# A fused attention and feed-forward layer: the opening rewritten to work in tile pairs, with two more engines in the layer norm and extra unit-matrix matmuls

## What is computed

```
xn  = (x - mean(x)) / sqrt(var(x) + 1e-5)            # per row of 512
lin(a, w, s) = (a @ sign(w).T) * mean(|w|, row) * s
q, k, v = lin(xn, wq, sq), lin(xn, wk, sk), lin(xn, wv, sv)
att = softmax(q @ k.T / 4) @ v                        # 4 query heads share a k/v head
ffn = (silu(xn @ (gate*sg).T) * (xn @ (up*su).T)) @ (down*sd).T
out = x + lin(att, wo, so) + ffn
```

## Time and profile before

| | |
|---|---|
| time, median of 3 runs | 505.62 us (503.99, 505.62, 506.27) |
| span of the profiled execution | 502.6 us |
| TensorE busy in the span | 479.6 us (95%) |
| VectorE busy | 417.2 us (83%) |
| ScalarE busy | 350.3 us (70%) |
| GpSimd busy | 94.4 us (19%) |

### The profile page before, as it was taken

One profiled execution on the slowest core, in us unless ns is written; L12 is line 12 of the kernel. 1 busy time (PEld: TensorE's weight loads), 2 busy tenths in 40 slices (PEclk: granted clock), 3 DMA queues, 4 the chain that ended last, 5 costly groups with the idle time before them and its releaser, 6 DMA issues.

```text
span 502.6 us, 10338 instructions
## 1 busy us (share of the span) xinstructions
PE 479.6 (95%) x4186; PEld 163.0 (32%) x4186; DVE 417.2 (83%) x487; ACT 350.3 (70%) x655; POOL 94.4 (19%) x138
## 2 busy tenths in 40 slices
PE   0899999999999999999999999999999999999996
PEld 0564444434332222222222222222222233333442
DVE  6879868676778999999999999999999955223986
ACT  1853643343229999999999999999999978874000
POOL 4212334534323000000000000000000113241021
PEclk9999999999999999999999999999999999999999
DMA  8862782641103802102102211111120034452321
GB/s 260 252 123 81 159 171 38 187 91 22 23 0 42 148 23 63 40 24 65 39 25 63 40 37 49 41 53 32 41 62 24 14 96 107 110 148 79 105 82 45
DMA packets 31302, 39.02 MB, mean 78 GB/s; under 512 B 6608, under 2 KB 20816, under 8 KB 31256
## 3 DMA queue, kind: packets, MB, share of 16 engines
q1 hardware_dynamic: 22232, 27.34, 19.0%
q0 software_dynamic: 8304, 10.95, 11.8%
q10 hardware_dynamic: 720, 0.08, 0.1%
HBM read 33.24 MB, written 10.35 MB: 87 GB/s over the span
## 4 chain that ended last, share of the span: by engine, by line
PE 86%; ACT 8%; DVE 3%; issue 1%; DMA 1%; SPq 0%; ACTq 0%; DVEq 0%
PE ps L1301 25%; PE ps L1131 19%; PE ps L1235 12%; PE ps L1140 8%; ACT room L705 6%; PE ps L1207 5%; PE ps L1194 5%; PE ps L1110 3%; PE ps L1335 3%; PE ps L1271 2%; ACT osb L716 1%; DMA hlo<-x 1%; DVE nmx L838 1%; PE ps L1048 1%; PE ps L1102 1%
## 5 line engine op out<-in xcount | busy, mean ns | idle before, releaser
L838 DVE TENSOR_REDUCE nmx<-ps 128x1 f32<-128x1024 f32 x248 | 284.6, 1216 | 14.5 <-PE ps L1140 14.2
L705 ACT ACTIVATE room<-ps 128x512 f32<-128x512 f32 x512 | 272.4, 598 | 20.9 <-PE ps L1271 11.0
L1301 PE MATMUL ps<-room,vcur 128*32 128x256 f32 (+1 forms) x1880 | 159.1, 410 | 4.3 <-ACT osb L716 4.1
L1140 PE MATMUL ps<-kA,qst 48*128 48x512 f16 x496 | 140.4, 382 | 0.0
L1235 PE MATMUL ps<-qst,kB 50*128 50x512 f16 x432 | 132.2, 382 | 0.8 <-DVE room L937 0.5
L1131 PE MATMUL ps<-room,wf 128*128 128x512 f16 x448 | 100.6, 379 | 0.0
L1301 PEld LDWEIGHTS ps<-room,vcur 128*32 128x32 f32 x1880 | 37.1, 108 | 100.8 <-issue 55.6
L686 ACT ACTIVATE room<-ps,gsc 128x512 f32<-128x512 f32 x28 | 19.2, 687 | 61.6 <-PE ps L1131 61.6
L1131 PEld LDWEIGHTS ps<-room,wf 128*128 128x128 f16 x448 | 42.4, 98 | 55.1 <-issue 7.2
L1235 PEld LDWEIGHTS ps<-qst,kB 50*128 50x128 f16 x432 | 26.8, 93 | 89.1 <-ACT room L705 79.8
L543 POOL TENSOR_TENSOR hlo<-room,hhi 128x512 f16<-128x512 f32 x28 | 34.1, 1217 | 87.4 <-ACT hhi L616 87.4
(11 more groups left out here) (136 smaller groups left out, 320.1 us busy)
## 6 DMA issues: line engine op xcount, KB each, us to landing
qst<-q_scratch SPq DMA_DIRECT2D x32, 192.0 KB, 3.6
o_scratch<-osb SPq DMA_DIRECT2D x16, 256.0 KB, 2.3
q_scratch<-parts SPq DMA_DIRECT2D x12, 256.0 KB
hlo<-x SPq DMA_DIRECT2D x8, 256.0 KB, 6.1
parts<-x POOLq DMA_DIRECT2D x8, 256.0 KB, 3.5
wf<-gate POOLq DMA_DIRECT2D x14, 128.0 KB, 3.9
wf<-up POOLq DMA_DIRECT2D x14, 128.0 KB, 6.0
wd<-down POOLq DMA_DIRECT2D x1, 1792.0 KB, 14.3
```

Of the source, the lines that this page charges most:

```text
L705: nc.scalar.activation(probs[:, s % 2, r, :], ps[:, bank_of(gp, s, i), :], ACT.Exp, scale=gam_reg[par][r]).then_inc(scores_free, 1)
L838: nc.vector.tensor_reduce(nmx[:, hf, idx:idx + 1], bank_pair(idx % 2), AX.X, ALU.max, negate=True).then_inc(rows_free, 1)
L1140: return nc.tensor.matmul(ps[:, 2 * (idx % 2) + b, :], qst[low:low + KROWS, par, hf, head, qt * P:(qt + 1) * P], kA[low:low + KROWS, par, ...
L1301: mm = nc.tensor.matmul(ps[32 * r:32 * r + 32, 7, of], vcur[:, par, key_tile(r, j), :], probs[:, s % 2, r, of], start=(j == 0 and part == ...
```

## The change

It touches only the first two stages. Layer norm goes by pairs of tiles in place of groups of four. VectorE keeps the statistics, the reciprocal and the normalisation of tiles 6 and 7. GpSimd does the Newton step and a shift of minus mean times reciprocal, seven instructions per pair, six of which follow the reciprocal one after the other. ScalarE normalises tiles 0 to 5 with that scale and shift (new step `A`), and loads its SiLU table early (new step `U0`). The gain steps `K0` and `K1` go from the front of TensorE's list to behind `G0` and `P0`. TensorE's `U0` and `G1` go ahead of `S0` and `Z0`. The small vectors are laid side by side in one array on the host and come in one transfer on SyncE's queue behind wk, as `svb` does behind wv. The first feed-forward load is issued by GpSimd between its pairs 1 and 2. And TensorE does 24 float32 matmuls of the unit matrix with itself into bank 5, which nothing else uses then, before the first transpose, and two more after each of the transposes of tiles 0 to 5.

```diff
-    pe_order = ("K0 K1 X0 X1 X2 X3 X4 X5 X6 X7 G0 P0 P1 S0 Z0 U0 Z1 G1 P2 Z2 P3 U1 F2 F3 F4 P4 P5 F5 F6 A0 F7 A1 A2 "
+    pe_order = ("X0 X1 X2 X3 X4 X5 X6 X7 G0 K0 P0 K1 P1 U0 G1 S0 Z0 Z1 P2 Z2 P3 U1 F2 F3 F4 P4 P5 F5 F6 A0 F7 A1 A2 "
...
-    dve_order = ("M0 M1 J0 M2 J1 M3 H0 M4 R0 M5 N0 N1 M6 M7 L0 H1 N2 R1 N3 N4 L1 N5 L2 N6 N7 L3 L4 L5 L6 L7 J2 S0 Z0 "
+    dve_order = ("M0 M1 M2 R0 M3 M4 R1 M5 M6 R2 L0 M7 L1 R3 L2 N6 N7 L3 L4 L5 J0 L6 L7 J1 J2 S0 Z0 "
...
-    act_order = ("D0 C0 C1 D1 N1 C2 N2 C3 N0 C4 B5 C5 C6 C7 B4 B2 B0 B1 B3 F0 E0 E1 F1 X0 X1 F2 E3 F3 V2 W0 X3 F4 E4 E5 "
+    act_order = ("D0 A0 D1 A1 C0 D2 C1 A2 A3 D3 C2 A4 C3 A5 N0 C4 C5 C6 C7 N1 N2 U0 B5 B4 B2 B0 B1 B3 F0 E0 E1 F1 X0 X1 F2 E3 F3 V2 W0 X3 F4 E4 E5 "
...
-    NORM_GROUPS = [(0, 4), (4, 8)]
+    PAIRS = [(t, t + 2) for t in range(0, TT, 2)]
...
             load_weights(wk, NH * D, wk_loaded)
+            sp.dma_start(vec[:, :], vecs).then_inc(vec_loaded, 16)
             load_weights(wq, 0, wq_loaded)
             load_weights(wv, NH * D + KV, wv_loaded)
+            sp.dma_start(svb[:, :], sv.to_broadcast([P, KV])).then_inc(svb_loaded, 16)
...
-            pool.wait_ge(x_loaded[TT - 1], 16)
-            load_ffn(0)
...
+            for t0, t1 in PAIRS:
+                if t0 == TT // 2:
+                    load_ffn(0)
+                of = slice(t0, t1)
+                pool.wait_ge(stats_ready, t1)
+                step(nc.gpsimd.tensor_scalar(half_var[:, of], mv[:, of, 1], EPS, -0.5, ALU.add, ALU.mult))
+                pool.wait_ge(inverse_ready, t1 // 2)
+                step(nc.gpsimd.tensor_tensor(newton[:, of], rstd[:, of], rstd[:, of], ALU.mult))
+                step(nc.gpsimd.tensor_tensor(newton[:, of], newton[:, of], half_var[:, of], ALU.mult))
+                step(nc.gpsimd.tensor_scalar(newton[:, of], newton[:, of], 1.5, None, ALU.add))
+                step(nc.gpsimd.tensor_tensor(rstd[:, of], rstd[:, of], newton[:, of], ALU.mult))
+                step(nc.gpsimd.tensor_tensor(shift[:, of], mv[:, of, 0], rstd[:, of], ALU.mult))
+                nc.gpsimd.tensor_scalar(shift[:, of], shift[:, of], -1.0, None, ALU.mult).then_inc(rstd_ready, 1)
...
-            act.dma_start(gsc[:, :], sg).then_inc(gains_loaded, 16)
-            act.dma_start(usc[:, :], su).then_inc(gains_loaded, 16)
-            act.dma_start(scqk[:, 0:QT], sq).then_inc(vec_loaded, 16)
-            act.dma_start(scqk[:, QT:QT + 1], sk).then_inc(vec_loaded, 16)
...
-                    if n == 0:
-                        act.dma_start(svb[:, :], sv.to_broadcast([P, KV])).then_inc(vec_loaded, 16)
+                elif kind == "U":
+                    nc.scalar.activation(warm[:, :], eps[:, :], ACT.Silu)
+                elif kind == "A":
+                    act.wait_ge(rstd_ready, n // 2 + 1)
+                    if n >= 4:
+                        act.wait_ge(xT_ready, n - 3)
+                    nc.scalar.activation(xn[:, n % 4, :], xin[:, n, :], ACT.Identity, bias=shift[:, n:n + 1],
+                                         scale=rstd[:, n:n + 1]).then_inc(xn_act_ready, 1)
...
-                ln_result(nc.vector.reciprocal(rstd[:, of], std[:, of]))
-                ln_result(nc.vector.tensor_tensor(newton[:, of], rstd[:, of], rstd[:, of], ALU.mult))
-                ln_result(nc.vector.tensor_tensor(newton[:, of], newton[:, of], half_var[:, of], ALU.mult))
-                ln_result(nc.vector.scalar_tensor_tensor(out=rstd[:, of], in0=newton[:, of], scalar=1.5, in1=rstd[:, of],
-                                                         op0=ALU.add, op1=ALU.mult))
+                nc.vector.reciprocal(rstd[:, of], std[:, of]).then_inc(inverse_ready, 1)
...
+            def keep_warm(n_):
+
+                for _ in range(n_):
+                    nc.tensor.matmul(ps[:, 5, 0:P], ident[:, :], ident[:, :], start=True, stop=True)
+
+            keep_warm(24)
...
                 mm.then_inc(xT_ready, 1)
+                if i < TT - 2:
+                    keep_warm(2)
```

More of the change, by code:

```diff
@@ L25, with layer_kernel @@
 LIFT = 16384.0
-def layer_kernel(nc, x, wq, wk, wv, wo, wq_rows, wk_rows, wv_rows, wo_rows, sq, sk, sv, so, gate, up, down, sg, su, sd, out,
+def layer_kernel(nc, x, wq, wk, wv, wo, wq_rows, wk_rows, wv_rows, wo_rows, sv, so, vecs, gate, up, down, sd, out,
                  q_scratch, k_scratch, o_scratch, r_scratch):
@@ L74, in layer_kernel @@
     T_AT = [n for kind, n in pe_order[:pe_order.index(("T", 0))] if kind == "F"][-1]
-    NORM_GROUPS = [(0, 4), (4, 8)]
+    PAIRS = [(t, t + 2) for t in range(0, TT, 2)]
+    ACT_NORM = [n for kind, n in act_order if kind == "A"]
+    DVE_NORM = [n for kind, n in dve_order if kind == "N"]
+    assert ACT_NORM + DVE_NORM == list(range(TT))
     SIGNS = [n for kind, n in act_order if kind == "N"]
@@ L181, in layer_kernel @@
         mv = sb("mv", [P, TT, 2], F32)
+        shift = sb("shift", [P, TT], F32)
         std = sb("std", [P, TT], F32)
@@ L204, in layer_kernel @@
         sgno = sb("sgno", [P, HC, H], F16)
-        scqk = sb("scqk", [P, QT + 1], F32)
+        vec = sb("vec", [P, 2 * FT + QT + 1], F32)
+        gsc, usc, scqk = vec[:, 0:FT], vec[:, FT:2 * FT], vec[:, 2 * FT:]
         cqk = sb("cqk", [P, QT + 1], F32)
@@ L263, in layer_kernel @@
         vec_loaded = sem("vec_loaded")
-        gains_loaded = sem("gains_loaded")
+        svb_loaded = sem("svb_loaded")
         sob_loaded = sem("sob_loaded")
@@ L274, in layer_kernel @@
         std_ready = sem("std_ready")
-        xn_ready = sem("xn_ready")
+        inverse_ready = sem("inverse_ready")
+        inverse_step = sem("inverse_step")
+        rstd_ready = sem("rstd_ready")
+        xn_act_ready = sem("xn_act_ready")
+        xn_dve_ready = sem("xn_dve_ready")
         xT_ready = sem("xT_ready")
@@ L531, in _, with step @@
             nc.gpsimd.memset(vext[:, :, :, :], 1.0).then_inc(consts_ready, 1)
-            pool.wait_ge(x_loaded[TT - 1], 16)
-            load_ffn(0)
+            steps = 0
+            def step(ins):
+                nonlocal steps
+                steps += 1
+                ins.then_inc(inverse_step, 1)
+                pool.wait_ge(inverse_step, steps)
+            for t0, t1 in PAIRS:
[11 more added lines that the diff above has]
+                nc.gpsimd.tensor_scalar(shift[:, of], shift[:, of], -1.0, None, ALU.mult).then_inc(rstd_ready, 1)
             pool.wait_ge(rows_q_loaded, 16)
@@ L682, in _ @@
                     if n == 0:
-                        act.wait_ge(gains_loaded, 16 * 2)
+                        act.wait_ge(vec_loaded, 16)
                     if n >= 2:
@@ L806, in hidden_factors @@
                 if stage == 0:
-                    dve.wait_ge(gains_loaded, 16 * 2)
+                    dve.wait_ge(vec_loaded, 16)
                     step(nc.vector.tensor_tensor(guprod[:, :], usc[:, :], gsc[:, :], ALU.mult))
@@ L944, in _ @@
                     dve.wait_ge(both_ready, 1)
+                    dve.wait_ge(svb_loaded, 16)
                     nc.vector.tensor_tensor(svb[:, :], ps[:, 7, KV:2 * KV], svb[:, :], ALU.mult).then_inc(factors_ready, 1)
@@ L1042, in _ @@
             pe.wait_ge(consts_ready, 1)
+            def keep_warm(n_):
+                for _ in range(n_):
+                    nc.tensor.matmul(ps[:, 5, 0:P], ident[:, :], ident[:, :], start=True, stop=True)
+            keep_warm(24)
             def transpose_x(i):
-                pe.wait_ge(xn_ready, i + 1)
+                if i in ACT_NORM:
+                    pe.wait_ge(xn_act_ready, ACT_NORM.index(i) + 1)
+                else:
+                    pe.wait_ge(xn_dve_ready, DVE_NORM.index(i) + 1)
                 if i >= 4:
@@ L1384 @@
         "wv_rows": rows(L0_attn_v_weight), "wo_rows": rows(L0_attn_o_weight),
-        "sq": columns(L0_attn_q_scale), "sk": columns(L0_attn_k_scale),
+        "vecs": np.ascontiguousarray(np.concatenate([columns(L0_ffn_gate_s), columns(L0_ffn_up_s), columns(L0_attn_q_scale),
+                                                     columns(L0_attn_k_scale)], axis=1)),
         "sv": row(L0_attn_v_scale), "so": row(L0_attn_o_scale),
         "gate": tiles(L0_ffn_gate_t), "up": tiles(L0_ffn_up_t), "down": turned(L0_ffn_down_t),
-        "sg": columns(L0_ffn_gate_s), "su": columns(L0_ffn_up_s), "sd": row(L0_ffn_down_s),
+        "sd": row(L0_ffn_down_s),
     }
```

21 lines of the change are left out of this document (7 added, 14 removed).

## The result

| | before | after |
|---|---|---|
| time, median of 11 runs | 503.99 us (503.74 to 507.49) | 507.93 us (506.23 to 511.01) |
| ratio after to before | | 1.0064 (95% interval 1.0045 to 1.0083) |
| profiled execution: time, span | not listed, 502.6 us | 507.22 us, 505.2 us |
| mean granted clock in it | 1.00 | 0.997 |

The changed kernel is 0.64% slower by the ratio, about 3.2 us; the two medians are 3.9 us apart. I had forecast 506.1 us, half a microsecond slower and so no change. The measured time lies in the range; the likeliest case did not come true, and to "slower by over 0.5%" I had given a chance of 0.20.

What follows compares the result with a forecast made beforehand. TensorE, 86% of the chain that ended last, was taken to bound the kernel, so opening shifts carry through. Terms -2.3 + 0.3 + 1.7 + 0.5 + 0.3 = +0.5 us on 505.62 gave 506.1 us, range 503.9 to 508.8.

Steps and rivals of the forecast that it cites:

- the likeliest case: Whole kernel: the forecast of no change, 505.0 to 507.6 us, chance 0.60.
- 1, up to P0: Opening up to P0: VectorE sheds work, GpSimd hops are added, P0 moves from 23.36 to 21.1 us, -2.3 us.
- 2, K1: Behind P0 on TensorE: K1's two records come in there, some 0.3 us of issue, +0.3 us.
- 3, the wait ahead of Z1: Factor chain: with U0 and G1 moved ahead, TensorE stands still from Z0's issue to Z1, +1.7 us.
- 4, U1: Between Z1 and U1: VectorE needs 8.1 us, TensorE has 7.6 without G1, so it waits +0.5 us.
- 5, F4: Ahead of F4: the step 2 product comes 9.0 us after `q_up`, 40 matmuls cover 8.6, so +0.3 us.
- both limits: P0 in the opening: VectorE's normalisation path (21.05) and the landing of G0's weights (21.1 to 21.2) both say 21.1 us.
- For P0 the clock is worth nothing more: Opening: full clock for transposes gives P0 no further gain, since GpSimd and VectorE set it.
- GpSimd was not slower than taken: Rival, opening: GpSimd steps of 0.50 us instead of 0.28 put P0 4.2 us later, 510.3 us; chance 0.15.
- The clock was held: Rival, opening: the low clock returns between sparse transposes, P0 up to 4 us later, 510 us, partly 508; chance 0.08.
- The covered factor chain: Rival, factor chain: the waits ahead of Z1, U1 and F4 do not arise, 503.6 us, 502 with quick GpSimd; chance 0.04.
- the opening is quicker: Rival, opening: GpSimd steps of 0.20 us, DMA dip wholly repaired, K1 hidden, 504.3 us, still no change; chance 0.13.

Runs made afterwards that it cites:

- two repeats: The changed kernel run again without any edit, on other jobs: medians 507.65 us (ratio 1.0050) and 508.08 us (ratio 1.0063).
- the combination: Changed kernel with old TensorE order, K0/K1 between X3 and X4, J0 to J2 around L2, first feed-forward load before pair 1, E0 before SiLU table: 503.34 us, ratio 0.9963.
- the first repeat of the changed kernel: The changed kernel once more without edits, on the chip of the next three runs: 507.65 us, ratio 1.0050.
- the last repeats: One-chip runs: changed kernel with TensorE's old order 505.89 us, changed kernel 508.08 us, kernel before 505.03 us, beside the combination, 503.34 us.

## Why the prediction was wrong in its sum and right in most of its parts

| term | forecast us | measured us | how |
|---|---|---|---|
| 1, up to P0 | -2.3 | -1.4 (-0.9 and -0.7 in two repeats) | P0 at 21.94, 22.42, 22.69 |
| 2, K1 | +0.3 | +0.4 | P0 to the end of P1: 7.32 for 6.90 |
| 3, the wait ahead of Z1 | +1.7 | +1.7 (idle 1.60) | v projection |
| 4, U1 | +0.5 | +0.6 (idle 0.43) | U1 |
| 5, F4 | +0.3 | +0.2 | start of attention |
| sum | +0.5 | +1.5 (+2.0, +2.3) | |

**Terms 2 to 5 held**, and so did the reason of term 3: the new order in the kernel before makes the same waits, and the order put back removes them. The changed kernel's loss is this order's. Its opening with its unit matmuls and the old order is no slower than before, 1.0000 and 1.0008.

**The step that failed is in term 1, that both limits meet at P0 = 21.1.** The pace of the GpSimd path was right, steps of 0.28 us, and so were its times, pair 1 done at 11.8 (12.1 forecast), pair 3 at 17.0 (17.2). But the times were right by luck, as two errors cancelled. The DMA dip is gone (125 to 367 GB/s), where I took half, and the statistics of tile 4 started at 7.71 us for 9.70 before. And ScalarE, whose work "lies beside this" in the prediction, stands in the path: its normalisation takes 0.81 us and not the half that I gave it, its list holds pair 1's square root behind the first normalisation, and VectorE's reciprocal waits 1.27 us for that. Of the 2.0 us by which tile 4 came earlier, 0.7 is left at the reciprocal (9.86 for 10.52), and the weights are issued behind it. No run took this wait out, so what it costs at P0 is not shown.

What set P0 in the end is the other limit, the landing of the weights: the second half was issued at 12.51 (12.4 forecast) and took 7.5 us, not the 7.0 of the earlier trace rows. It landed at 20.0 instead of 19.4. G0 from 20.10 takes 1.73, K0 0.11: P0 at 21.94. I had taken a duration measured in the old schedule as a constant and left no room for it, at the place where both limits stood 0.1 us apart; in the six profiles with the load in this place it is 6.8 to 8.1. The wait recurs in four of the other five, 0.8 to 1.2 us; the combination, which loads one pair earlier, has none. In the fifth, the first repeat of the changed kernel, P0 started 0.14 us behind VectorE's last low half; the changed kernel's own was done at 21.32, so P0 would have been near 21.5 without the wait (an estimate). Of the 0.8 us that term 1 missed, the weights make about 0.5.

**Where tile 2's arrival came in.** The statistics of tile 2 started between 6.0 and 7.1 us in the six profiles; the transposes of tiles 6 and 7 followed 12.0 us behind them in each, and P0 at 21.9 to 23.2, where the weights' landing adds a scatter of its own. In the old opening the chain hangs on tile 3, whose statistics started at 8.3 to 8.6 us in four profiles, with P0 14.8 to 15.0 behind. By pairs, `R0` behind `M2` hangs on tile 2, whose landing scatters over 1.1 us. I had priced the new hops and not the new dependence. The -1.4 of the profile is the best of the six; -0.7 is their middle.

**The unit matmuls.** "For P0 the clock is worth nothing more" is wrong by 0.3 to 1.2 us: at the low level the transposes come into the chain of each pair, and G0 runs its first matmuls there. It was right of the kernel before (P0 at 23.43 with them, 23.36 without).

**From the span to the time.** I took the time as 3.0 us above the span. An execution's own time lies 2.0 to 2.2 above its span in every kernel with the new opening, and 1.7 to 1.9 with the old; my 3.0 was the scatter of three runs. So some 0.3 us of the loss lies outside the span. It is not the unit matmuls, since it is there without them and not in the kernel before with them, nor the place of the SiLU table load, which the combination moved; which part of the new opening brings it stays open. Forecast span 503.1, measured 505.2; forecast distance 3.0, measured 2.0: the second error took off half of the first.

**Why the time lay in the range all the same.** That was luck in part. I had put the +0.5 us on 505.62, the median of three executions of the kernel before; the median of eleven is 503.99. Laid around that, the same range would have ended at 507.2, below the 507.93 measured. And the case that came, slower by 0.64%, was neither of my two slow rivals, but the smaller gain of term 1, 0.3 us outside the span, and a part that goes along with the clock at the start of attention, for which I had no term.

**The sum of the loss.** Start of attention +1.5 to +2.3, outside the span +0.3: about 2.3 us. Executions with a mean granted clock of 0.998 or more say the same: medians of 506.4 to 506.8 for the changed kernel in its three sets of runs (3, 6 and 1 executions), 504.0 to 504.5 for the one before. The remaining 0.9 us of the measured 3.2 go along with the clock: 3.4 us of the low level cost 1.2 at the start of attention, and the mean was 0.997 or less in 23 of 33 executions of the changed kernel against 34 of 92 of the kernel before. But on the chip of the last repeats the kernel before had 11 of 35 in one set and 7 of 12 in another, so it is not shown that the change makes it more frequent. Of most of these executions only the mean is known, not where the clock fell. Why it falls there stays open.

The rivals: GpSimd was not slower than taken. Its two-input instructions of 128x2 take 0.19 to 0.20 us, against 0.16 for one of 128x4 on VectorE. The Trainium skill (GPSIMD Engine Reference, Engine selection) gives a factor of about two for two inputs; these rows, of 2 and 4 elements per partition, show 1.2. The clock was held in the changed kernel's opening: its unit matmuls go from 421 to 275 ns each between 7.5 and 8 us, and the transposes stay at the quick pace. It need not be: in the profile with the early load and G1 first it was low from 13.4 to 16.8 us, unit matmuls and all. The covered factor chain did not come. That the opening is quicker was half so: the dip was repaired, and the wait for ScalarE and the weights took that back.

## What to carry to other kernels

Before matmuls are moved ahead of a small step, look what they cover behind it: a hop from TensorE to VectorE and back costs its whole length (here 1.6 us) once nothing stands in it, whatever the engines' busy shares say. When an opening is made quicker, the next limit can be a load that was hidden (here 0.5 us of P0): price it with a duration from the new traffic and leave a margin, and issue it where its queue holds nothing that the critical chain needs. Look also at the order of the engine that is given new work: a small step that others wait for, here a square root, must not stand behind a long one. And count from the landing of the tile on which the chain now hangs before two profiles are compared: between the changed kernel and the one without unit matmuls it made 1.6 us of a difference of 2.4.

## What the runs showed of the hardware

- Five small loads, some with packets of 4 bytes, stood beside a dip of the DMA to 125 GB/s between 5 and 6 us, and to 94 to 191 in the other three profiles of the old opening. Laid side by side on the host as one load of 16.5 KB, they leave 367 GB/s in the same microsecond, and 283 to 346 in the other nine of the new one. The median time from issue to landing of an x tile was 5.8 to 6.1 us in the old opening, and 4.2, 5.2 and 5.0 in the changed kernel. The packets were changed together with the queue they go by, so their size alone is not shown to be the cause.
- The clock was at the low level (1.2 GHz) for 3.4 us in four profiles, and for 10.2 us in two, at the start of attention, behind waits of TensorE of no more than 0.45, 0.19 and 0.20 us, in kernels with and without unit matmuls and with either order; the same waits stood there in profiles in which it held. The short stretches cost 0.9 to 1.3 us, the long ones 3.8 and 4.0.
- A normalisation of 128x512 on ScalarE, with scale and bias per row, takes 0.81 us; its copy of the same size out of PSUM to float16 takes 0.58. VectorE's normalisation takes 0.54 (two in a row 1.00).
